# One bank instead of two for the first products of a remainder tile in a fused attention and mixture-of-experts kernel

## The reference, cut to what matters

```python
logits = jnp.einsum('btd,de->bte', x, Wg) + bg
top2_vals, top2_idx = jax.lax.top_k(logits, 2)
scores = jax.nn.softmax(top2_vals, axis=-1)
...
h = jnp.einsum('btd,edh->bteh', x, W1) + b1[None, None]
h = jax.nn.gelu(h, approximate=False)
y = jnp.einsum('bteh,ehd->bted', h, W2) + b2[None, None]
out = jnp.einsum('bted,bte->btd', y, combine)
return _layer_norm(x + out, gamma, beta)
```

## Time and profile before

| | |
|---|---|
| median of three runs | 1296.34 us |
| profiled execution, its own time | 1300.37 us |
| its span, from first to last instruction | 1298.6 us |
| PE busy | 1131.4 us (87% of the span) |
| DVE busy | 902.9 us (70%) |
| ACT busy | 790.0 us (61%) |
| POOL busy | 650.6 us (50%) |
| mean granted TensorE clock | 0.910 of full speed |

### The profile page before, as it was taken

The page is one execution under the profiler, slowest core; times in us unless marked ns, Lnnn a source line. Parts: engine busy times, 40 slices in busy tenths (PEclk is TensorE's granted clock), DMA queues, the critical chain, the costliest instruction groups (busy, mean ns, idle before and its releaser), DMA issues.

```text
span 1298.6 us, 23742 instructions
## 1 busy us (share of the span) xinstructions
PE 1131.4 (87%) x8184; PEld 1039.9 (80%) x8184; DVE 902.9 (70%) x1943; ACT 790.0 (61%) x1597; POOL 650.6 (50%) x581
## 2 busy tenths in 40 slices
PE   3789999998869999999988971999999999999950
PEld 2688787887858888888877861999999999999940
DVE  5677887676666666666637755787878787787847
ACT  3756566644235565565627640887878777787836
POOL 2435443443253666555443776255665745445326
PEclk8658999879999999999997865999999999999985
DMA  6544332221333778666647742568888776666649
GB/s 223 182 148 151 136 139 98 74 98 50 119 119 115 195 220 233 177 166 173 155 87 240 224 138 74 175 137 197 187 184 204 172 193 174 165 156 185 176 87 241
DMA packets 147497, 206.69 MB, mean 159 GB/s; under 512 B 29137, under 2 KB 121425, under 8 KB 140337
## 3 DMA queue, kind: packets, MB, share of 16 engines
q1 hardware_dynamic: 111376, 161.87, 38.1%
q0 software_dynamic: 35040, 42.75, 19.2%
q10 hardware_dynamic: 960, 0.54, 0.1%
HBM read 154.58 MB, written 50.53 MB: 158 GB/s over the span
## 4 chain that ended last, share of the span: by engine, by line
PE 70%; DVE 11%; ACT 6%; issue 5%; POOL 5%; DMA 2%; SPq 0%; ACTq 0%; DVEq 0%; POOLq 0%
PE quad L2029 14%; PE pb L2048 14%; PE quad L1200 13%; PE pb L1215 7%; PE quad L298 4%; PE pb L352 4%; PE pb L366 2%; POOL dSL L1882 2%; PE pb L264 1%; ACT Dm L839 1%; DVE Dm L527 1%; PE quad L2001 1%; PE quad L2023 1%; PE pb L1185 1%; PE quad L1480 1%
## 5 line engine op out<-in xcount | busy, mean ns | idle before, releaser
L2224 POOL DMA_INDIRECT dOUT<-y,es x71 | 118.9, 1675 | 192.4 <-DVE y L2130 179.5
L2048 PE MATMUL pb<-wh,hh 128*128 128x256 f32 x568 | 164.4, 289 | 1.1 <-DVE hl L2117 1.1
L2048 PE MATMUL pb<-wh,hl 128*128 128x256 f32 x568 | 160.7, 283 | 0.0
L2048 PE MATMUL pb<-wl,hh 128*128 128x256 f32 x568 | 160.6, 283 | 0.0
L1346 POOL DMA_INDIRECT dACC<-ye,idxJ x64 | 100.2, 1566 | 103.7 <-ACT ye L1310 54.7
L2186 ACT ACTIVATE gl<-quad,b1c 128x256 f32<-128x256 f32 (+1 forms) x312 | 124.6, 450 | 24.5 <-PE quad L2023 14.4
L2117 DVE TENSOR_TENSOR hl<-gl,hh 128x512 fp32r<-128x512 f32 (+1 forms) x156 | 99.6, 642 | 44.6 <-ACT hh L2191 42.5
L2029 PE MATMUL quad<-xh,wh 128*128 128x256 f32 x512 | 104.5, 286 | 8.2 <-ACT gl L2186 6.7
L2205 POOL DMA_INDIRECT xs<-dZ,es x71 | 95.9, 1351 | 28.0 <-issue 18.3
L2048 PEld LDWEIGHTS pb<-wh,hh 128*128 128x128 f32 x568 | 108.8, 192 | 1.3 <-DVE hl L2117 1.3
L2048 PEld LDWEIGHTS pb<-wl,hh 128*128 128x128 f32 x568 | 108.9, 192 | 0.0
(11 more groups left out here) (293 smaller groups left out, 3356.3 us busy)
## 6 DMA issues: line engine op xcount, KB each, us to landing
w2r<-in_W SPq DMA_DIRECT2D x39, 1024.0 KB, 5.8
MB<-dM SPq DMA_DIRECT2D x16, 1024.0 KB, 5.7
wraw<-in_Wg SPq DMA_DIRECT2D x16, 512.0 KB, 6.5
wraw<-in_Wu SPq DMA_DIRECT2D x16, 512.0 KB, 7.9
wraw<-in_Wd SPq DMA_DIRECT2D x16, 512.0 KB, 5.3
W<-in_W SPq DMA_DIRECT2D x8, 1024.0 KB, 10.7
w1p<-in_W SPq DMA_DIRECT2D x7, 1024.0 KB, 7.5
b2c<-in_b SPq DMA_DIRECT2D x39, 128.0 KB, 3.1
```

Of the source, the lines that this page charges most:

```text
L2048: ins = pe.matmul(bank.t[:, 0:256], a_[s][:, c, 128 * tt:128 * tt + 128], b_[n % 3][:, 256 * c:256 * c + 256], start=half == 0 and m == 0, ...
L2224: g.indirect_dma_start(out=dOUT[:, :], out_offset=bass.IndirectOffsetOnAxis(ap=es[i % 6][:, tt, 1:2].bitcast(U32), axis=0), in_=y1[i % 2][ ...
```

## The change

For a remainder, a half takes one bank and not two: all four blocks go side by side into it, each at its own 128 columns. The bank is taken at `q_` = 0 and counts as free after the gelu of `q_` = 1. Full tiles are as before. On ACT both gelu groups of such a half wait for the signal that TensorE raises behind the fourth block; before, the first group waited only for the second block. The numbers of matmuls, activations and casts are the same.

```diff
                 for q_ in range(2):
-                    bank, was = ab4.take((i, half, q_), a_t, "gelu", i, half, q_)
-                    if was:
-                        pe.wait_ge(*was)
+                    if q_ == 0 or not whole(i):
+                        bank, was = ab4.take((i, half, q_), a_t, "gelu", i, half, 1 if whole(i) else q_)
+                        if was:
+                            pe.wait_ge(*was)
...
-                                ins = pe.matmul(bank[:, TS * c:TS * c + width(i)], w1p[remainder(i) % 2][:, k, 512 * half:512 * half + 512][:, fs],
+                                ins = pe.matmul(bank[:, fs], w1p[remainder(i) % 2][:, k, 512 * half:512 * half + 512][:, fs],
                                                 xf[remainder(i) % 2][:, k, :], start=k == 0, stop=k == 1)
...
-                        a.wait_ge(*pe_t.of("up", i, half, q_))
+                        a.wait_ge(*pe_t.of("up", i, half, 1 if whole(i) else q_))
...
-                            ins = a.activation(g_[:, c, 0:width(i)], ab4.of(i, half, q_)[:, TS * c:TS * c + width(i)], ACT.Gelu, bias=b1c[i % 6][:, cc:cc + 1])
+                            c0 = 2 * q_ + c
+                            pre = ab4.of(i, half, 0)[:, 128 * c0:128 * c0 + 128] if whole(i) else ab4.of(i, half, q_)[:, TS * c:TS * c + TS]
+                            ins = a.activation(g_[:, c, 0:width(i)], pre, ACT.Gelu, bias=b1c[i % 6][:, cc:cc + 1])
```

## The result

| | before | changed |
|---|---|---|
| median, us (runs) | 1301.8 (5) | 1314.81 (5) |
| lowest and highest, us | 1295.75, 1302.15 | 1309.81, 1316.72 |
| ratio, 95% interval | | 1.0109 [1.0082, 1.0136] |
| profiled execution, its own time, us | 1300.37 | 1309.81 |
| its span, us | 1298.6 | 1308.1 |

The kernel is slower by 1.1%, some 14 us (0.0109 x 1301.8). The forecast was +5.8 us, with a range up to 1306.0 us. Its direction was right, its size was less than half of what was measured. (Two more runs of the kernel before moved its median from the 1296.34 us from which the prediction started to 1301.8.) All ratios are times over those of the kernel before, and leave out the two far slower executions on record, of 2811 and 4564 us.

A forecast was written before the change was run, and what follows sets the result against it. The prediction took the fourth stage to run at PE's pace, losing time only at remainders through an ACT and DVE chain ending in `wl`. 5.3 + 0.9 - 0.4 = +5.8 us gave 1302.1 us, range 1299.0 to 1306.0.

The forecast's parts named there:

- Banks, gain 0: One bank wait fewer on PE in each of 14 halves; gain 0, bounded by up to 6.7 us.
- The releaser of PE: PE's wait before the next tile is for `wl`; rival: a bank held by ACT's gelu, 1289.6 us, chance 0.04.
- First half, 0.89 us each: ACT's first gelu of a remainder starts 0.89 us later, PE's wait grows equally; six remainders, 5.3 us.
- Second half, 0: ACT comes late to this gelu, so waiting for four blocks costs 0; rival that both halves pay: 1308.8 us, chance 0.04.
- Register load, 0.4 us back: Loading the next expert's number at the first three remainders may quicken; bounds nothing to 1.1 us, taken as 0.4 us off.
- Sum of these: Six first halves 5.3 us, plus last remainder's later end 0.9, minus register load 0.4: +5.8 us.
- the clock's term: Rival: PE's longer idle time before the next tile lowers the clock behind six waits; 1319 us, chance 0.03.
- The price of the clock: If the clock fell, 24 matmuls behind each of six waits at half speed would add 17 us.
- What was to show it wrong: PE's wait before L2029 stays, shrinks or grows by over 1 us each, or the clock leaves 1.00 behind it.

The follow-up runs named there:

- the wait alone: The kernel before, with two banks for a half of a remainder, but ACT's first gelu waits for all four blocks in both halves; ratio 1.0122 [1.0087, 1.0158].
- the first half alone: The changed kernel with one bank and the wait for four blocks only in the first half of a remainder; ratio 1.0121 [1.0089, 1.0153].

## Why the prediction was wrong

- *Banks, gain 0.* Right: the wait without the bank costs the same (1.0122), and the second half with its bank costs nothing that the times show (1.000).
- *The releaser of PE.* Right: `wl` and not the gelu that the profile names, read from a start 0.01 us before the named releaser's end.
- *First half, 0.89 us each.* Right: 1.98 us to the first gelu, and 56.53 - 55.64 = 0.89 us in the distances that have no fall. One detail was off: PE comes to its wait 0.06 us later than before, counted from L2024, so the wait grows by 0.83 and not by 0.89. The prediction had left down(r, 0) a margin of 0.11 us; that this margin was too small is likely and was not tested.
- *Second half, 0.* Right, and shown by leaving the first half as it was (1.000 and equal distances).
- *Register load, 0.4 us back.* Mis-sized. It was near the far bound of 1.1 us: the waits at the first three remainders grew by only 0.47, 0.44 and 0.55 us and not by 0.83, so about 1.0 us came back. The load at the first took 282 ns.
- *Sum of these.* 5.3 + 0.9 - 1.0 = 5.2 us, against 13.4 + 0.9 - 9.1 = 5.2 us measured. What is missing from the forecast is the clock's 9.1 us.
- *The step that failed* is the clock's term, which the sum and the range put at nothing: "The granted clock was 1.00 (2.4 GHz) over the stretch with 1.31 us", "0.50 (1.2 GHz) where PE did nothing for 5 us", "in between I have no row of this stage", chance 0.03. The waits were to grow into just this gap, at six places, and the range ended at 1306.0 as if it were closed. In its place the runs showed a fall to 0.50 behind waits of 1.78 us, 1.51 us a time and 9.1 us for six. A gap without a row should have been taken as a bound from both sides, as the register load was. The Trainium skill ("TensorE: Matmul & The Clock Gate", section HAM oscillation) was cited beside it for gaps "of this kind". It does warn of PE's idle gaps, but of longer ones: by its rule 1.78 us would have been harmless. Here the measurement decides.
- *The price of the clock* was wrong too, the other way: 24 products at half speed behind each wait, 17 us. The fall came over 1 us after the first of them, so it covered only a part.
- *What was to show it wrong* did: the clock left 1.00 behind the wait.

The gap in the rows was one of the fourth stage only. The same trace of the kernel before has waits of the new length in earlier stages, where PE's work is less continuous and its matmuls have other shapes. Behind one of 1.93 us the clock fell within 2 us; behind one of 2.40 us it did not. PE's timeline and the windows behind both waits:

```profile
222.46 0.37 PE L338 MATMUL pb<-rthl,hTh 128*128 128x32 f32 x2 [1.93 <-DVE hTl L606]
...
372.04 0.36 PE L366 MATMUL pb<-wsh,hhs 128*128 128x256 f32 x1 [2.40 <-POOL hls L1015]
```

```profile
223.00:225.00 2.00, 2.00 (x11) 1.54 (x10) 2.00 (x4) 1.97 (x3) 1.29 (x1) 0.81 1.01 389
225.00:227.00 2.00, 2.00 (x10) 1.65 (x8) 1.93 (x6) 0.57 (x2) 0.00 (x0) 0.50 1.01 422
...
372.00:374.00 2.00, 1.96 (x16) 1.99 (x17) 2.00 (x2) 1.40 (x2) 1.82 (x1) 1.00 0.00 0
374.00:376.00 2.00, 1.31 (x11) 1.11 (x10) 2.00 (x4) 0.00 (x0) 1.70 (x2) 1.00 0.22 66
```

These rows could not have told which way the new waits would go, but they speak against a chance of 0.03 and a range without the fall.

## What to carry to other kernels

A delay of 0.9 us on a helper engine cost 2.4 us a time (58.04 - 55.64), because the clock fell behind TensorE's longer wait. When an edit makes TensorE's idle time longer, look for a wait of the new length anywhere in the trace. If none stands there, or if the clock fell behind one of them, put the fall into the range. The fall doesn't show in busy shares: look at the granted clock behind the wait, and at the length of equal matmuls. Where such a wait can't be avoided, try one useless product in it; here it held the clock. And check a releaser that the profile names against its end time and the order of waits in the code.

## What had not been expected of the hardware

- Before the tile behind a remainder, the clock fell at 22 of 24 places where PE had waited 1.77 to 1.79 us (four profiles: the changed kernel twice, the wait alone, the first half alone), and at none of 60 where it had waited 1.56 us or less (the ten other profiles). The two places without a fall had the same wait (1.78 and 1.77 us), so the length alone doesn't decide.
- Other places say the same. Behind the 1.93 us wait of an earlier stage the clock fell within 2.1 us in all fourteen profiles, and behind the 2.40 us wait in none. Behind PE's last wait of the stage, 1.96 to 1.98 us in eight profiles, it fell within 1.5 us in four of them and not in the other four. What else decides was not settled.
- One extra product (two records, 0.39 us) in the wait of 1.78 us was enough. Whether its own work or the 1.55 us left behind it holds the clock was not told apart.
- The fall comes late: PE resumed at 911.44 us at full speed, and the slow products began at 912.98 us. The clock stood at 0.50 over products that followed each other without a gap.
- ACT's register load from SBUF took 647 ns at the first remainder of the kernel before and 282 ns at that of the changed kernel, where it comes 0.9 us later behind the remainder's products. Whether this shift makes the difference, and whether transfers cause it, was only argued from the DMA share.
